# Splitting the last output store of a residual-projection kernel over two DMA queues

## What is computed

```python
x_mean = jnp.mean(x, axis=1, keepdims=True)
fused = jnp.concatenate([x, x_mean * ones_L, hidden[:, None, :] * ones_L], axis=-1)   # hidden = [cond, cond]
out = x + jax.nn.relu(jnp.einsum('bld,do->blo', fused, W) + b)                        # W is 1536 x 512
```

## Time and profile before

| | us |
|---|---|
| Median of 3 runs | 103.4 (103.25 to 103.8) |
| The profiled execution's own time | 103.63 |
| Its span, first to last instruction | 101.7 |
| TensorE busy | 97.2 (96% of the span) |
| VectorE busy | 83.0 (82%) |
| ScalarE, GpSimd busy | 47.1 and 38.9 |

### The profile page before, as it was taken

The page is one execution under the profiler, slowest core; times in us unless marked ns, Lnnn a source line. Parts: engine busy times, 40 slices in busy tenths (PEclk is TensorE's granted clock), DMA queues, the critical chain, the costliest instruction groups (busy, mean ns, idle before and its releaser), DMA issues.

```text
span 101.7 us, 1713 instructions
## 1 busy us (share of the span) xinstructions
PE 97.2 (96%) x523; PEld 78.5 (77%) x523; DVE 83.0 (82%) x148; ACT 47.1 (46%) x116; POOL 38.9 (38%) x35
## 2 busy tenths in 40 slices
PE   5989999999999999999999999999999999999980
PEld 2348999988888786888888886888888886888870
DVE  3172789899899899999999984999999993996670
ACT  3285435895418279496397001874744003710000
POOL 1029800000000002999848500568578059950000
PEclk9999999999999999999999999999999999999999
DMA  1999999999999998999999388000591690299994
GB/s 38 269 303 290 273 268 282 273 251 266 318 256 231 269 251 221 246 234 226 345 331 286 106 195 219 0 0 0 113 267 32 134 259 20 67 283 273 248 325 144
DMA packets 35438, 21.39 MB, mean 210 GB/s; under 512 B 2020, under 2 KB 33128, under 8 KB 35432
## 3 DMA queue, kind: packets, MB, share of 16 engines
q1 hardware_dynamic: 33848, 20.13, 77.4%
q10 hardware_dynamic: 1584, 1.18, 3.9%
HBM read 12.91 MB, written 8.39 MB: 209 GB/s over the span
## 4 chain that ended last, share of the span: by engine, by line
PE 90%; DMA 4%; ACT 1%; DVE 1%; ACTq 0%; issue 0%
PE ps_y L472 77%; PE ps_y L573 4%; PE ps_y L575 4%; PE ps_y L574 4%; DMA xa<-in_x_dram 4%; PE ps_mean L491 1%; PE ps_const L540 1%; ACT xh L267 1%; DVE ps_xt L341 1%; ACT w1h L260 1%; DVE w L462 0%; ACTq L160 0%; PE ps_y L596 0%
## 5 line engine op out<-in xcount | busy, mean ns | idle before, releaser
L240 POOL TENSOR_TENSOR xa<-xa,back 128x512 f32 (+1 forms) x26 | 33.5, 1318 | 44.7 <-DVE back L354 44.7
L472 PE MATMUL ps_y<-xh,w1h 128*128 (+2 forms) x128 | 43.6, 368 | 0.4 <-ACT w1h L260 0.3
L472 PE MATMUL ps_y<-xl,w1h 128*128 (+2 forms) x128 | 43.0, 363 | 0.0
L472 PE MATMUL ps_y<-xh,w1l 128*128 (+2 forms) x128 | 42.8, 363 | 0.0
L267 ACT ACTIVATE xh<-ps_xt 128x512 fp32r<-128x512 f32 (+1 forms) x36 | 19.7, 549 | 17.4 <-DVE ps_xt L341 17.4
L472 PEld LDWEIGHTS ps_y<-xh,w1h 128*128 128x128 f32 x128 | 22.6, 189 | 5.4 <-issue 1.1
L347 DVE TENSOR_TENSOR xl<-ps_xt,xh 128x512 fp32r<-128x512 f32 (+1 forms) x36 | 22.1, 617 | 4.9 <-ACT xh L267 4.9
L472 PEld LDWEIGHTS ps_y<-xh,w1l 128*128 128x128 f32 x128 | 22.6, 189 | 3.8
L472 PEld LDWEIGHTS ps_y<-xl,w1h 128*128 128x128 f32 x128 | 22.7, 189 | 3.6
L341 DVE STREAM_TRANSPOSE ps_xt<-xa 128x512 f32<-128x512 f32 (+1 forms) x36 | 22.3, 642 | 3.6 <-DMA xa<-in_x_dram 3.3
L285 ACT ACTIVATE relu_t<-ps_y,bias 128x512 f32<-128x512 f32 x20 | 13.5, 686 | 16.8 <-DVE bias L388 15.3
(11 more groups left out here) (35 smaller groups left out, 37.1 us busy)
## 6 DMA issues: line engine op xcount, KB each, us to landing
xa<-in_x_dram SPq DMA_DIRECT2D x60, 128.0 KB, 3.8
out_dram<-xa SPq DMA_DIRECT2D x28, 256.0 KB, 4.1
w<-in_L_cond_W_dram SPq DMA_DIRECT2D x4, 256.0 KB, 5.5
w<-in_L_cond_W_dram SPq DMA_DIRECT2D x2, 512.0 KB, 6.7
w<-in_x_dram SPq DMA_DIRECT2D x4, 256.0 KB, 4.6
out_dram<-w SPq DMA_DIRECT2D x3, 256.0 KB, 3.4
xa<-in_x_dram ACTq DMA_DIRECT2D x4, 128.0 KB, 4.4
w<-in_L_cond_W_dram SPq DMA_DIRECT2D x4, 64.0 KB, 3.4
```

What stands on the lines that cost most here:

```text
L240: nc.gpsimd.tensor_tensor(rows, rows, back[:, t], ALU.add).then_inc(added, 1)
L472: return nc.tensor.matmul(ps_y[:, t, ls], lhs, rhs, start=start, stop=stop, skip_group_check=True)
```

## The change

`store_last` gets the partitions to be stored as an argument. The first half of row block 3 (128 partitions x 256 columns) is issued by SP instead of ScalarE. The second half becomes two DMAs of 64 partitions x 256 columns, 64 KB each: partitions 0 to 63 by SP, 64 to 127 by ScalarE. SP waits for one more store at the end.

```diff
-        def store_last(eng, r, cols, added_steps):
+        def store_last(eng, r, cols, added_steps, rows=slice(0, P)):
             eng.wait_ge(last_added, added_steps)
-            eng.dma_start(out_rows[LAST, :, r, cols], last_x[:, r, cols]).then_inc(stored, 16)
+            eng.dma_start(out_rows[LAST, rows, r, cols], last_x[rows, r, cols]).then_inc(stored, 16)
...
             for r in range(NR - 1):
                 store_last(sp, r, slice(0, D), r + 1)
-            store_last(sp, NR - 1, slice(D // 2, D), NR + 1)
-            sp.wait_ge(stored, 16 * (NQ * LAST + NR + 1))
+            store_last(sp, NR - 1, slice(0, D // 2), NR)
+            store_last(sp, NR - 1, slice(D // 2, D), NR + 1, slice(0, P // 2))
+            sp.wait_ge(stored, 16 * (NQ * LAST + NR + 2))
...
             nc.scalar.activation(last_hl[:], last_bias[:, D // 2:D], ACT.Copy).then_inc(last_hi_ready, 1)
-            store_last(act, NR - 1, slice(0, D // 2), NR)
+
+            store_last(act, NR - 1, slice(D // 2, D), NR + 1, slice(P // 2, P))
```

## The result

| | before | changed |
|---|---|---|
| Median of 22 runs each | 103.45 us (102.97 to 104.21) | 103.94 us (103.54 to 104.53) |
| Ratio | | 1.0044, 95% interval 1.0025 to 1.0064 |
| Profiled execution, its span | 103.63, 101.7 | 103.54, 101.6 |

The change makes the kernel slower by 0.44%, 0.46 us (0.26 to 0.66). It is a small loss but a clear one, on the side that I had given 0.09, and just outside the range of 102.9 to 103.9.

What follows compares the result with a forecast made beforehand. TensorE, busy 96%, bounds the kernel; only 2.45 us behind the last addition can change. SP's issue 0, pair's start 0, extra increment +0.02 gave 103.65 profiled, so 103.4 us forecast (0.68), range 102.9 to 103.9.

Steps and rivals of the forecast that it cites:

- the side that I had given 0.09: Whole kernel: slower by more than about 0.5% of the time (0.52 us), given a chance of 0.09.
- The place: End of the kernel: the change can act only on the 2.45 us behind VectorE's last addition.
- a fault in the base: Behind the last addition: the prediction is wrong in its base if those 2.45 us change by over 0.5.
- The first half moves to SP, cost 0: Row block 3's first half: SP, free by then, issues it at 98.21 in 0.46 us, done before 99.28; cost 0.
- The bounds ... within -0.12 to 0: Last store: a 64-partition DMA's first packet comes earlier than 0.83 us after issue, by -0.06, within -0.12 to 0.
- the lagging engine: Last store: one DMA engine, some 0.4 us behind with old work, sets the end; one extra increment costs it +0.02 us.
- Side by side: Last two stores: SP and ScalarE both issue at 99.28 or 99.29, taking 0.33 to 0.38 us each.
- the first rival: Kernel's end: not always set by a late DMA engine, so the earlier start counts; faster, 102.9 to 103.35 us; chance 0.13.
- Rival 2, SP late: SP's last two issues: if long behind a full queue, the second ends late; 103.45 to 103.85 us; chance 0.10.
- Rival 3, half of the partitions moves slower: Last store's data: 265 GB/s instead of 389 if partitions are the cause, +0.15 us, or 103.55; chance 0.09.
- The rule that splitting isn't worth it: Last store: disjoint partition halves share the same 16 engines and serialize, saving only issue time; sum 0 to -0.06 us.

## Why the prediction was wrong, step by step

- **The place.** Right. Only the 2.45 us behind the last addition matter, and that is where the loss lies: 2.71 against 2.47, less than the 0.5 that was named as a fault in the base.
- **The first half moves to SP, cost 0.** Right: issued at 97.88 in 0.33 us (0.46 had been taken), and the move alone gave 1.0001.
- **"The bounds ... within -0.12 to 0" for the start of the pair.** This is the step that failed. I took the first packet of a 64-partition DMA to lie between that of 1 partition (0.70 to 0.73 us) and that of 128 (0.83), because the two were the nearest rows. It was at 1.21, with an issue of 0.56 instead of 0.33. The sum had the start at 0, hidden by the lagging engine, with an earlier start of -0.06 behind it; measured is +0.38. The trace of before has not one 64-partition DMA among its issues, so the two ends bounded nothing but a trend that I had assumed. The bound had no side above zero, and so the range was too short on the slow side.
- **Side by side.** The issues ran side by side, but not what follows them: ScalarE's packets began 0.28 us behind SP's. Its first packet came 1.48 us after its issue, 0.29 more than when it issued 0.46 us later than SP. The sum had no term for this. The split into 96 and 32 has the same 0.28 and no loss in time that the runs can tell, so it isn't enough alone.
- **The lagging engine.** I let it hide whatever the other engines did. It was the state of some executions: in 4 of the 17 traces (the kernel before, the ones that store only 32 and only 96 partitions, and the split into 96 and 32) a 2 KB packet of older stores ended after the first packet of the last store. In the changed kernel's trace, and in that of the whole store by ScalarE, all engines had caught up before the last store came. Where it is absent there is no cover of 0.4 us. The prediction named this as the first rival and looked only for what it would gain. Nor would the cover have been enough: the lagging engine of before ended 1.73 us behind the last addition, the two halves 1.96.
- **Rival 2, SP late.** It ended on the right side with the wrong cause, which is luck. Its condition was a full queue; the issues that should have been long (97.88) were short, and the last were long with the queue nearly empty.
- **Rival 3, half of the partitions moves slower.** The mechanism is there (63 ns against 46), and its size is 0.07 us per half, below the 0.15 given. Its sign showed as well: 190 and 166 GB/s in the last stretches, under 300, though the engines were not all busy (shares 0.80 and 0.65). My argument against it was that the two halves are in flight together and reach all the ports. For the most part they weren't together, being 0.28 us apart; that this is why it failed is argued, not shown.
- **The rule that splitting isn't worth it** ("DMA: Bandwidth & Descriptors", "Rules for kernel authors" in the Trainium skill) was right in its advice. I had worked out 0 to -0.06 us from it; what came was a loss, with causes that it doesn't name.

Put together against the clean whole store, ScalarE's: its last packet ends 1.43 us behind the last addition, the changed kernel's 1.96. The 0.53 between them are +0.31 for the first packet (1.23 against 0.92 behind the addition), +0.28 for the second half behind the first, and -0.07 since half as many packets, though slower ones, follow the second's start. This is one trace of each, and the whole store's is the most favourable of those without a split. Against the trace of before, with its lagging engine, the difference is 0.24. The timed difference of 0.46 us (0.26 to 0.66) lies between the two, as it would if some executions of the kernel before have such an engine and some have not; how many is not known.

Open is why a DMA of 64 partitions takes longer to issue and to start. The traces show the count at which it happens. It happens with either number of bytes and at each place tried, with an issue of 0.64 us instead of 0.55 at partitions 32 to 95. Counts other than the six were not tried. The traces don't show what the queue does in that time. Whether loads have it too was not tried. No version that stores everything was found faster than the kernel before; the whole store by either engine, and the 96 + 32 split, can't be told from it.

## What to carry to other kernels

Most of what lies behind the last addition is not data moving: of the clean whole store's 2.17 us its packets took 0.52, and the rest is issue, start and landing. A split lets fewer packets follow each start but adds a second start, and of the splits tried none gained. What less data alone would save is not settled here, since the halves that were stored alone had the late start of 64 partitions. An operation of a shape that the trace doesn't have can't be bounded by its neighbours above and below; give it a price on both sides, or measure that shape by itself first. A cover that one execution shows, like one late DMA engine, is worth nothing until another execution shows it as well.

## What the runs showed of the hardware

- At the end of this kernel, a store of 64 partitions took SP 0.55 to 0.64 us to issue and ScalarE 0.53 to 0.56, and its first packet came 1.2 to 1.3 us after the issue's start (1.48 for ScalarE's beside SP's). Last stores of 32, 48, 80, 96 and 128 partitions, with no other issued at the same moment, took 0.33 to 0.38, and 0.83 to 0.89.
- 1 KB packets of a store took 63 ns from partitions 0 to 63 and 46 ns from 32 to 95, and from 0 to 127. 2 KB packets took 144 ns from 0 to 63 and 84 from 0 to 127.
- Two stores issued at the same moment by SP and ScalarE do not start together: ScalarE's packets began 0.28 us behind SP's for 64 and 64 partitions, 0.28 for 96 and 32, 0.19 for 128 and 128 partitions of 512 bytes, and 0.09 for 32 and 32.
- From the end of the last packet to the end of the span it was 0.72 to 0.76 us in 15 of the 17 traces, whatever the store, and 0.84 and 0.88 us in the other two (only 32 partitions, and the split by columns).
